# First routed stage: half of the chunks prepared inside the loop, weights split in parts, second-half gates in fewer tiles

## The reference

```python
x = x + 0.5 * _L0_ffn_ref(_layernorm(x, axis=-1), gate_w, experts_gate_up, ...)

logits = x_flat @ gate_w.T
scores = jax.nn.softmax(logits, axis=-1)
_, topk_ids = jax.lax.top_k(scores, 2)
in_topk = jax.nn.one_hot(topk_ids, E).sum(axis=1)
w = scores * in_topk
gu = jnp.einsum('nh,eih->nei', x_flat, experts_gate_up)
g, u = (gu[..., :I], gu[..., I:])
h = jax.nn.silu(g) * u
expert_out = jnp.einsum('nei,ehi->neh', h, experts_down)
out = jnp.einsum('neh,ne->nh', expert_out, w)
shared = silu(x_flat @ shared_gate_w.T) * (x_flat @ shared_up_w.T) @ shared_down_w.T
out = out + sigmoid(x_flat @ shared_expert_gate_w.T) * shared
```

## Time and profile before

| | us |
|---|---|
| median of 3 runs | 1439.98 |
| lowest, highest | 1439.55, 1446.33 |
| profiled execution | 1449.88 |
| its span, first to last instruction | 1448.1 |

### The profile page before, as it was taken

The page is one execution under the profiler, slowest core; times in us unless marked ns, Lnnn a source line. Parts: engine busy times, 40 slices in busy tenths (PEclk is TensorE's granted clock), DMA queues, the critical chain, the costliest instruction groups (busy, mean ns, idle before and its releaser), DMA issues.

```text
span 1448.1 us, 26900 instructions
## 1 busy us (share of the span) xinstructions
PE 1393.1 (96%) x9296; PEld 1115.4 (77%) x9296; DVE 1124.1 (78%) x2500; ACT 977.7 (68%) x1765; POOL 637.9 (44%) x601
## 2 busy tenths in 40 slices
PE   6999999999999999999999998999989999989998
PEld 5788888766666665778888877999967777769998
DVE  7777776698888898578777786787788889856765
ACT  6666666557777776765666667877656666658886
POOL 6566666600000000146666665677512323356664
PEclk9999999999999999899999999999999999989999
DMA  6000000000000000002000001000000000000001
GB/s 184 1 2 1 1 1 1 1 1 1 1 1 1 1 1 2 1 1 90 1 16 1 15 2 58 2 2 1 1 1 1 2 2 1 2 1 2 16 16 30
DMA packets 13317, 16.82 MB, mean 12 GB/s; under 512 B 768, under 2 KB 10496, under 8 KB 12928
## 3 DMA queue, kind: packets, MB, share of 16 engines
q1 hardware_dynamic: 13184, 15.11, 3.4%
HBM read 13.01 MB, written 2.10 MB: 10 GB/s over the span
## 4 chain that ended last, share of the span: by engine, by line
PE 82%; DVE 9%; ACT 3%; issue 3%; POOL 1%; DMA 1%; SPq 0%; DVEq 0%; POOLq 0%; ACTq 0%
PE PS L865 19%; PE PS L892 9%; PE PS L2125 9%; PE PS L2142 8%; PE PS L1034 5%; PE PS L1054 5%; PE PS L1042 4%; PE PS L1013 2%; PE PS L1438 2%; PE PS L1463 2%; PE PS L1472 2%; PE PS L1448 1%; PE PS L1496 1%; PE PS L1420 1%; DVE AR L1242 1%
## 5 line engine op out<-in xcount | busy, mean ns | idle before, releaser
L764 POOL TENSOR_TENSOR RR<-AR,RR 128x512 fp32r<-128x512 f32 x150 | 194.1, 1294 | 136.2 <-ACT RR L793 130.7
L836 ACT ACTIVATE AR<-PS 128x512 f32<-128x512 f32 x224 | 133.9, 598 | 146.4 <-PE PS L865 143.5
L728 DVE TENSOR_TENSOR AR<-AR,PS 128x512 f32<-128x512 f32 x224 | 153.4, 685 | 101.5 <-PE PS L865 90.1
L1159 ACT ACTIVATE AR<-PS 128x512 f32<-128x512 f32 x256 | 152.3, 604 | 85.7 <-PE PS L1042 85.0
L1242 DVE TENSOR_REDUCE AR<-PS 128x2 f32<-128x512 f32 x256 | 172.3, 686 | 21.5 <-PE PS L1034 20.7
L865 PE MATMUL PS<-XHI,WG 128*128 128x512 f32 x448 | 179.4, 400 | 0.2
L865 PE MATMUL PS<-XHI,WU 128*128 128x512 f32 x448 | 175.5, 392 | 2.0 <-DVE AR L728 2.0
L734 DVE TENSOR_TENSOR AR<-AR,PS 128x512 f32<-128x512 f32 x224 | 154.0, 687 | 11.0 <-PE PS L881 2.9
L2125 PE MATMUL PS<-XHI,SL 128*128 128x256 f32 x576 | 135.1, 290 | 4.4 <-DVE XTR L2293 2.5
L2396 POOL CAST SL<-ZW 128x1024 fp32r x96 | 100.3, 1044 | 86.4 <-PE PS L2142 85.7
L2220 ACT ACTIVATE PS<-PS 128x1024 f32<-128x1024 f32 x96 | 96.8, 1009 | 58.6 <-PE PS L2125 58.3
(11 more groups left out here) (303 smaller groups left out, 3581.6 us busy)
## 6 DMA issues: line engine op xcount, KB each, us to landing
X<-in_x SPq DMA_DIRECT2D x4, 512.0 KB, 6.5
out_x<-X SPq DMA_DIRECT2D x4, 512.0 KB, 3.2
AR<-in_w SPq DMA_DIRECT2D x1, 1792.0 KB, 11.7
AR<-in_zone_down SPq DMA_DIRECT2D x7, 256.0 KB, 4.8
XT<-in_w SPq DMA_DIRECT2D x1, 1608.0 KB, 6.6
AR<-in_zone_up SPq DMA_DIRECT2D x6, 256.0 KB, 5.4
XT<-in_sel SPq DMA_DIRECT2D x1, 896.0 KB, 6.7
SM<-in_small SPq DMA_DIRECT2D x1, 857.5 KB, 7.0
```

Of the source, the lines that this page charges most:

```text
L728: v.tensor_tensor(PRD[:, m % 2, :], SIL[:, m % 2, :], bank(2 + m % 2), ALU.mult).then_inc(S.prod, 1)
L764: g.tensor_tensor(HL[k % 3], GAT[:, m % 2, :], HH[k % 3].bitcast(F32), ALU.subtract).then_inc(S.h_lo, 1)
L836: act.activation(SIL[:, m % 2, :], bank(m % 2), ACT.Silu).then_inc(S.silu, 1)
L1159: act.activation(PT[:, g % 2, k, 2 * jp:2 * jp + 2, :], bank(2 + m % 2).rearrange("p (j q) -> p j q", j=2), ACT.Exp, scale=SC0).then_inc(S ...
```

## The change

In the first stage only (n = 0), except for waits that later stages find fulfilled:

- The front runs over chunks 0 to 3. Chunks 4 to 7 are turned in the loop of chunk 0, at its tiles 0, 3, 5 and 7, and projected at its tiles 3, 6, 8 and 10 (`behind`); they use bank 7 and bank 5. ScalarE's normalising of chunks 6 and 7 is in halves at tiles 1, 2, 4 and 5, its high copies and VectorE's copies at the tile after each turn. Normalising of chunks 4 and 5 stays in the front.
- The rest of the first-half gates stands behind the front of VectorE in one piece. The first weights are turned after `up(0, 1)` instead of ahead of it, into banks 4 and 5, and ten fillers follow at tile 1.
- GpSimd does the selectors after all of WU and counts `G.split` up with each part of WU's low part. WD is split in quarters: one ahead of the loop, three behind its tiles 1, 4 and 7 (`split_down`). TensorE waits for the part that it needs.
- The second-half gates: `gate_logits` at tile 12, exponentials at 14, `gate_share` at 15, three operations each at 16, 17, 18 and 19; the weights at 20 and 22 as before.

```diff
-            for c in range(3 if n else 0, NC):
+            for c in range(3 if n else 0, front(n)):
...
-            logits_out(n, NC - 1)
+            logits_out(n, front(n) - 1)
+            if n == 0:
+                gate_first(v, n, gates, 0, 0)
+                gate_best(v, n, gates, 0, 1)
+                gate_first(v, n, gates, 0, 1)
+                gate_weights(v, n, gates, 0)
...
+        FRONT_C = NC // 2
+        TURN_AT, LOGITS_AT = (0, 3, 5, 7), (3, 6, 8, 10)
+
+        def front(n):
+
+            return NC if n else FRONT_C
+
+        def turned_in(n, c):
+
+            return bank(c % 4) if c < front(n) else bank(7)
+
+        def logits_in(n, c):
+
+            return bank(4 + c % 2 if c < front(n) else 5)[:, 0:TPC * GC]
+
+        def behind(n, c, m, at, later=0):
+
+            if n or c or m - later not in at:
+                return None
+            return FRONT_C + at.index(m - later)
...
             for t in range(TPC):
-                last = pe.transpose(turned_in(c)[:, t * P:(t + 1) * P], XN[:, c % 2, t, :], ident)
+                last = pe.transpose(turned_in(n, c)[:, t * P:(t + 1) * P], XN[:, c % 2, t, :], ident)
...
-            wait(pe, S.lg_dve, c - 1, D.lg_dve)
+            wait(pe, S.lg_dve, c - 1 if c < front(n) else c, D.lg_dve)
...
             for t in range(TPC):
-                last = pe.matmul(logits_in(c)[:, t * GC:(t + 1) * GC], XTC[:, c % 2, t * P:(t + 1) * P], T.gw,
+                last = pe.matmul(logits_in(n, c)[:, t * GC:(t + 1) * GC], XTC[:, c % 2, t * P:(t + 1) * P], T.gw,
                                  start=True, stop=True)
             last.then_inc(S.lg_pe, 1)
...
             act = nc.scalar
             act.wait_ge(S.nbias, D.nbias + (2 if c * TPC >= part_of(n, 1).start else 1))
             wait(act, S.tr, c - 1, D.tr)
-            for t in range(on_act(n, c)):
+            ts = range(first, min(first + count, on_act(n, c)))
+            for t in ts:
                 k = c * TPC + t
                 last = act.activation(XN[:, c % 2, t, :], X[:, k, :], ACT.Identity, scale=RSTD[:, k:k + 1],
                                       bias=NBIAS[:, k:k + 1])
-            last.then_inc(S.xna, 1)
+            if ts.stop == on_act(n, c):
+                last.then_inc(S.xna, 1)
 
...
-        def wt_place(r):
-
-            return (bank(7), slice((r + 1) * 512, (r + 2) * 512)) if r else (bank(6, 2), slice(0, 1024))
+        def wt_place(n, r):
+
+            return (bank(7), slice((r + 1) * 512, (r + 2) * 512)) if r else (bank(6 if n else 4, 2), slice(0, 1024))
...
-            if MT0 * c + m == 5:
+            if MT0 * c + m == (5 if n else 14):
                 gate_exps(n, 1)
...
             v = nc.vector
             k = MT0 * c + m
-            if k == 2:
+            if k == (2 if n else 12):
                 gate_logits(v, n, ch, 1)
-            if k in (6, 7):
+            if n == 0 and k == 15:
+                gate_share(v, n, ch, 1)
+            if n == 0 and k in (16, 18):
+                gate_best(v, n, ch, 1, k // 18)
+            if n == 0 and k in (17, 19):
+                gate_first(v, n, ch, 1, k // 19)
+            if n and k in (6, 7):
                 gate_share(v, n, ch, 1, ((0, 1), (2,))[k - 6])
-            if 8 <= k < 11:
+            if n and 8 <= k < 11:
                 gate_best(v, n, ch, 1, 0, (k - 8,))
-            if 11 <= k < 14:
+            if n and 11 <= k < 14:
                 gate_first(v, n, ch, 1, 0, (k - 11,))
-            if 14 <= k < 17:
+            if n and 14 <= k < 17:
                 gate_best(v, n, ch, 1, 1, (k - 14,))
-            if 17 <= k < 20:
+            if n and 17 <= k < 20:
                 gate_first(v, n, ch, 1, 1, (k - 17,))
...
                 keep_busy(pe, bank(3), 6)
-            for c in range(4 if n else 0, NC):
...
                 if c > 0:
                     wait(pe, S.xlo, c - 3, D.xlo)
...
                 normed_in(n, 1)
-            for c in range(3 if n else 0, NC):
...
+                    if behind(n, c, m, TURN_AT, 1):
+                        copy_in(n, behind(n, c, m, TURN_AT, 1))
+                        low(n, behind(n, c, m, TURN_AT, 1))
+                    if behind(n, c, m, LOGITS_AT, 1):
+                        logits_out(n, behind(n, c, m, LOGITS_AT, 1))
                     v.wait_ge(S.silu, D.silu + k + 1)
...
 
+        def split_down(g, q):
+
+            w = MT0 * P
+            at = slice(q * w // 4, (q + 1) * w // 4)
+            hi, lo = (W.rearrange("p m h -> p (m h)")[:, at] for W in WD)
+            raw = AR[:, 2048 + 2 * w:2048 + 3 * w][:, at]
+            g.tensor_copy(hi, raw).then_inc(G.zeroed, 1)
+            g.wait_ge(G.zeroed, 4 + q)
+            g.tensor_tensor(lo, raw, hi.bitcast(F32), ALU.subtract).then_inc(G.split, 1)
...
+                    if n == 0 and k in (1, 4, 7):
+                        split_down(g, 1 + k // 3)
...
+                    if behind(n, c, m, TURN_AT, 1):
+                        copies_in(n, behind(n, c, m, TURN_AT, 1))
+                    if n == 0 and c == 0 and m in (1, 2, 4, 5):
+                        normed_in(n, 6 + m // 4, (0, 2)[m in (2, 5)], 2)
...
+            def split_part(n, c, m, up):
+
+                if n == 0 and c == 0:
+                    pe.wait_ge(G.split, 2 + min(m // 4, 2) + m // SHARED if up else 1)
+
             def product(out, w, m, c, sem):
 
+                split_part(n, c, m, w is WU)
...
-                    pe.wait_ge(S.lg_dve, D.lg_dve + NC)
+                    pe.wait_ge(S.lg_dve, D.lg_dve + (NC if s else front(n)))
+                    pe.wait_ge(G.split, 6)
...
-                if k == 0:
-                    pe.wait_ge(G.split, 2)
+                if n == 0 and c == 0:
+                    pe.wait_ge(G.split, 7 + ((m + 1) * P - 1) // (MT0 * P // 4))
...
+                if c == 1:
+                    pe.wait_ge(S.xlo, D.xlo + NC)
...
+                    if behind(n, c, m, TURN_AT):
+                        turn_in(n, behind(n, c, m, TURN_AT))
+                    if behind(n, c, m, LOGITS_AT):
+                        logits(n, behind(n, c, m, LOGITS_AT))
+                    if n == 0 and first and m == 1:
+                        keep_busy(pe, bank(6), 10)
...
-            pe.wait_ge(G.split, 1)
-            pe.wait_ge(S.xlo, D.xlo + NC - 1)
+            pe.wait_ge(S.xlo, D.xlo + front(n) - 1)
+            if n == 0:
+                logits(n, front(n) - 1)
             up(0, 0)
-            logits(n, NC - 1)
-            wt_turn(n, 0)
-            pe.wait_ge(S.xlo, D.xlo + NC)
+            if n:
+                logits(n, front(n) - 1)
+                wt_turn(n, 0)
+            pe.wait_ge(S.xlo, D.xlo + front(n))
             up(0, 1)
+            if n == 0:
+                wt_turn(n, 0)
...
                 for at in range(0, TILES0, 4):
                     m = slice(at, min(at + 4, TILES0))
-                    g.tensor_tensor(tiles(W[1])[:, m], dealt(i)[:, m], tiles(W[0])[:, m].bitcast(F32), ALU.subtract)
-                last = g.tensor_tensor(W[1][:, routed:w], RAW[:, i * w + routed:(i + 1) * w], W[0][:, routed:w].bitcast(F32),
-                                       ALU.subtract)
-                if i == 0:
-                    g.wait_ge(G.raw_in, 16 * (2 + len(DOWN_RUNS)))
-                    g.tensor_copy(SEL[:, 0:P].rearrange("p (e t) -> p e t", e=E0),
-                                  RAWS[:, 0:routed].rearrange("p (e i) -> p e i", e=E0)[:, :, 0:PER])
-                    g.tensor_copy(SEL[:, P:2 * P], RAWS[:, routed:routed + P])
-            last.then_inc(G.split, 1)
...
+                    last = g.tensor_tensor(tiles(W[1])[:, m], dealt(i)[:, m], tiles(W[0])[:, m].bitcast(F32), ALU.subtract)
+                    if i:
+                        last.then_inc(G.split, 1)
+                g.tensor_tensor(W[1][:, routed:w], RAW[:, i * w + routed:(i + 1) * w], W[0][:, routed:w].bitcast(F32),
+                                ALU.subtract).then_inc(G.split, 1)
+            g.wait_ge(G.raw_in, 16 * (2 + len(DOWN_RUNS)))
+            g.tensor_copy(SEL[:, 0:P].rearrange("p (e t) -> p e t", e=E0),
+                          RAWS[:, 0:routed].rearrange("p (e i) -> p e i", e=E0)[:, :, 0:PER])
+            g.tensor_copy(SEL[:, P:2 * P], RAWS[:, routed:routed + P]).then_inc(G.split, 1)
+            split_down(g, 0)
```

More of the change, by code:

```diff
@@ L475, in turn_in @@
             pe = nc.tensor
-            wait(pe, S.xlo, c - 3, D.xlo)
+            wait(pe, S.xlo, c - 3 if c < front(n) else c, D.xlo)
             if on_act(n, c) < TPC:
@@ L496, in logits, with normed_in @@
             for t in range(TPC):
-                last = pe.matmul(logits_in(c)[:, t * GC:(t + 1) * GC], XTC[:, c % 2, t * P:(t + 1) * P], T.gw,
+                last = pe.matmul(logits_in(n, c)[:, t * GC:(t + 1) * GC], XTC[:, c % 2, t * P:(t + 1) * P], T.gw,
                                  start=True, stop=True)
             last.then_inc(S.lg_pe, 1)
-        def normed_in(n, c):
+        def normed_in(n, c, first=0, count=TPC):
```

(4 more changed lines are left out.)

27 lines of the change are left out of this document (8 added, 19 removed).

## The result

| | kernel before | changed kernel |
|---|---|---|
| median | 1443.58 us (9 runs) | 1446.79 us (9 runs) |
| ratio of the runs, 95% interval | | 1.0032 (1.0016 to 1.0048) |
| profiled execution, its span | 1449.88, 1448.1 | 1445.54, 1443.4 |

The change makes the kernel slower by 0.32%, 4.6 us (2.3 to 6.9): within the 0.5% of the prediction's "same", but clearly not faster. The prediction was 2.7 us over a median of three runs, 1439.98. That it does is luck in part: by the traces, chunk 1 of the loop, which was to start 1.5 us earlier than before, starts 3 us later or more.

A forecast was written before the change was run, and what follows sets the result against it. TensorE, busy 96% of the span, was taken as the bound. To the median of 1440.0 us came 1.9 for late gates outweighing the front's gain and 1.0 for the clock: 1442.9, say 1442.7 us, range 1436 to 1447.

The forecast's parts named there:

- same: Outcome for the whole kernel: within about 0.5%, 7.2 us, of no change, between 1432.8 and 1447.2 us; chance 0.90.
- Part 1: Shorter front before the loop: first up product at 25.0 us, tile 2 at 32.1 instead of 38.7, 6.6 us earlier.
- Part 2: Work moved into chunk 0 of the loop: turns, logits and waits leave chunk 1 1.5 us earlier, of the 6.6.
- 24.3 + 5.0 + 3.3: Tile 2 to chunk 1 on TensorE: usual work 24.3 us, moved turns and logits 5.0, two added or lengthened waits 3.3.
- The first hole: In chunk 0, TensorE's gate product waits from 33.4 to 34.7 us for the low copy of the turned weights: 1.3 us.
- Part 3: Denser late gates on VectorE, tiles 15 to 19: TensorE waits 4.0 us; turn at tile 23 at 89.8, 1.9 late.
- 0.35 + 0.35 + 0.60 a group: VectorE's three late-gate operations a tile: one reduction, one while GpSimd waits, one slowed by GpSimd's work; 1.3 us with gaps.
- Clock: One stretch at the lower clock level expected between 30 and 42 us, costing 1.0 us, between 0 and 3.6.
- (a): Rival: the late gates fit and cost TensorE nothing, so the gain before chunk 1 stays; 1437 to 1439 us, chance 0.22.
- (b): Rival: chunk 0 of the loop swallows the moved work in existing holes and the 6.6 us stay; 1433.4 us, chance 0.06.
- (c): Rival: the clock stays low through chunk 0, to 58 us, at least 8 us more; 1449 and above, chance 0.06.
- (d): Rival: late gate weights or first-half gates keep the front from shortening; 3 us late gives 1446 us, chance 0.08.

The follow-up runs named there:

- no_fillers: The changed kernel without the ten fillers behind the first turn in the loop; ratio to the kernel before 1.0054.
- the reordered version: Changed kernel with late gates spread, no ten fillers, and ScalarE's and VectorE's preparation of chunks 4 to 7 behind the tile's SiLU and product; ratios 0.9990 and 0.9999.
- dense_alone: The kernel before with only the late gates of the change (logits at tile 12, exponentials at 14, three operations a tile at 15 to 19); ratio 1.0024.
- the pair without picks: Kernel before and changed kernel, each without the twelve operations picking the two best experts for chunks 2 to 7, one copy instead; ratios 1.0007 and 1.0008.
- spread: The changed kernel with late-gate picks spread over tiles 16 to 24 and the first late turn of the weights at tile 25 instead of 23; ratio 1.0015.

## Why the prediction was right and wrong

**Part 1, right as a chain, missized in two terms.** The chain (low part of the gate weights, first up product, weights of the first half) came as worked out where the front was warm: 24.87 and 29.50 against 25.0 and 29.5. (For the second of these numbers the slow stretch did by chance what the predicted wait should have done, as said above.) The two terms: ten fillers were put at 1.2 us and took 2.15, because I read the eight rows of four filler calls as eight fillers. And a cold front wasn't thought of: the rows of before showed 0.43 us a turn, and I took that for the front's constant. In both traces of the changed kernel tile 2 came at 35.6 instead of 32.1, 1.0 of it from the fillers, 2.1 from the cold front, the rest from the slow stretch at 28.5. In the times the fillers are nothing (no_fillers); a cold front was met in kernels with either front.

**Part 2, the step that failed.** It ends with chunk 1 at 64.7 against 66.2, "**1.5 us earlier**, of the 6.6". Chunk 1 started at 69.2 and 70.8, later than before instead of earlier, and in the five traces of versions that keep the order of the change and whose front wasn't slow up to 24 us it starts at 67.5 to 69.4. From tile 2 to chunk 1 I had 24.3 + 5.0 + 3.3 = 32.6 us; it took 33.6 and 35.2. The turns and logits were cheaper than I had them (0.35 and 0.81 us from start to start, 4.3 in all). The first hole was filled by the fillers; the second, 2.0 predicted, is 1.88. That makes 30.5. What is missing is, first, the slow stretch that follows the hole, 3.3 us at the lower level or, in the second trace, 6.8 us, on full work: 1.7 and 3.4 us, estimated as half of its length. Second, some 1.3 us of small losses between the tiles, for which I had no term; the second trace of before, without a slow stretch, has them too (27.0 us for 24.3 of work, with waits of 0.68, 0.56 and 0.21). The 43 added waits on the split counter show no cost: a steady tile takes 2.04 us in the changed kernel too (67.18 to 69.22).

The cause of that hole is the one the prediction named, VectorE's copy and low part ahead of the product of tile 1 and ScalarE's work ahead of the turned weights; the reordered version takes it away, and with it the hole and the slow stretch, 5.9 us by chunk 1. I had put that down as two waits of 3.3 us, with one slow stretch of 1.0 us for the whole stage, and not asked what the clock does behind each of them.

**Part 3, right in kind, too dear in size.** The step "this is what I expect to decide" is borne out as a cost of its own by dense_alone (1.0024) and the pair without picks, and by spread against after in the traces. It was not the only one that decided: by chunk 1 the changed kernel is already 3.0 us behind in the first trace. Predicted were 25.1 us from tile 14 to the turn and 4.0 of waiting; it took 24.35 and 24.37, with 2.44 of waiting at the turn. The rows that show why it was a little less: VectorE's operations on 192 columns take 0.35 or 0.36 throughout, and GpSimd's tile beside them 1.45 instead of 1.30.

```profile
78.40 0.36 DVE L589 TENSOR_TENSOR AR<-AR 128x192 f32<-128x192 f32 x1
...
78.79 0.36 DVE L591 TENSOR_TENSOR AR<-AR,SM 128x192 f32<-128x192 f32 x1
```

```profile
69.25 1.29 POOL L805 TENSOR_TENSOR RR<-AR,RR 128x512 fp32r<-128x512 f32 x1 [0.74 <-ACT RR L836]
...
78.84 1.45 POOL L805 TENSOR_TENSOR RR<-AR,RR 128x512 fp32r<-128x512 f32 x1 [1.03 <-ACT RR L836]
```

My 0.35 + 0.35 + 0.60 a group was the wrong way round in one place: beside these groups GpSimd starts last, and it is GpSimd that is slowed. In the earlier trace rows VectorE started while GpSimd was at work, and was slowed.

ScalarE's tables stand as assumed, and the exponential follows its load after 1.30 us, not 2.66 as the Trainium skill has a switch (ScalarE: Activation LUTs, What ACT_TABLE_LOAD costs):

```profile
69.19 1.28 ACT L568 ACT_TABLE_LOAD   x1
...
70.49 0.36 ACT L568 ACTIVATE AR<-AR 128x192 f32<-128x192 f32 x1
...
72.30 0.60 ACT L883 ACTIVATE AR<-PS 128x512 f32<-128x512 f32 x1
```

**Clock, missized.** I took 1.0 us for one stretch. There were three in each trace, against one and none in the traces of before: in the front, in the loop, and after the 2.44 us wait at tile 23, where in the first trace four transposes take 1.02 us and tile 24 to tile 28 takes 9.6 us instead of 8.5. The last two cost some 3 us in the first trace (1.7 in the loop, 1.5 here). I had counted the waits and left out what follows the last of them.

**The rivals.** (a), the gates fit, is refuted by dense_alone. (b) likewise. (c), a clock low through chunk 0, did not come: the longest stretch was 10 us, in no_fillers, and 45.4 to 69.2 of the changed kernel reads 1.00. Its sum has a slip: 10.6/2 is the cost of 10.6 us spent at the lower level, not of 10.6 us of full-speed work. (d), a late front, came in part, by chance of the clock.

**The sum.** At tile 28 the changed kernel is 7 to 10 us behind in the traces where the forecast has 2.9, with its 1.0 for the clock. In the first trace 3.0 of the 7.1 are there at chunk 1, and 4.0 come between chunk 1 and tile 28. The runs say 4.6 and 6.6. That the traces show more than the times is partly the slow stretch of the next stage; how much of it is chance is the part that stays open.

## What to carry to other kernels

Work moved onto a full engine is paid in full (4.3 us of turns and logits here), so its gain must come from the time that was freed; ask first what the engine waits for at the new place, and put the moved preparation behind that, not ahead of it. A wait on a full matrix engine costs its own length and then, where the clock falls behind it, some 1.5 to 3.5 us more here; it doesn't fall behind every wait. Below half a per cent, compare marks inside the stage over several traces, and expect the rest of the program to move by more than the change.

## What the runs showed that was not expected

- A preparation put ahead of what TensorE waits for cost 5.9 us by chunk 1, more than twice the waiting that it added, because a slow stretch followed.
- The front of 12 to 24 us runs cold (1.06 to 1.11 us for four transposes) in some executions and warm (0.60 to 0.66) in others of the same instructions, while the record of the granted clock says 1.00 in both.
- Where VectorE's two-operand operations on 192 columns and GpSimd's on 512 meet in these rows, the one that starts later is slowed: 0.35 to 0.60 us for VectorE, 1.30 to 1.45 for GpSimd.
- A filler call (a float32 product of 128x128) is two matmuls in the rows, 0.215 us together; a float32 transpose is one.
- Slow stretches of 7 to 20 us in the next routed stage, in which TensorE was busy the whole time (17.00 of 17.00 us at 0.51): in three of the traces the clock stayed down under steady work for as long as the longest stretch of the first stage (10 us) or longer.
